# Products of constants in TensorE's waits, in the prologue and in the last sequence's expert part

## What is computed

```python
x = x + attn(layernorm(x));  x = x + ffn(layernorm(x))

def attn(x):                                     # linear-attention form with decays and levels
    q, k, v = (x @ W.T).reshape(b, t, H, 128)    # for Wq, Wk, Wv
    g = -softplus(x @ Wg.T + bg);  lam = softplus((x @ Wdl.T) + Lparam)
    G = cumsum(g, axis=1)
    A = (q k^T / sqrt(128)) * exp(G_t - G_s) * lam[level(t - s)]      # s <= t
    out = (A @ v).reshape(b, t, H * 128) @ Wo.T + x
    return layernorm(out) * ln_g + ln_b

def ffn(x):
    gate = softmax(x @ Wg + bg); keep the two largest, divided by their sum
    return sum_e gate_e * (We[e] @ x + be[e])
```

## Time and profile before

| | |
|---|---|
| median of 3 runs | 1558.06 us (1557.87 to 1558.11) |
| profiled execution | 1560.17 us, its span 1558.40 us |
| TensorE busy (matmul) | 1448.6 us, 93% of the span |
| ScalarE, VectorE, GpSimd busy | 1164.9, 1024.3, 886.7 us |
| chain that ended last | TensorE 68%, ScalarE 11%, GpSimd 9%, VectorE 7% |

### The profile page before, as it was taken

One profiled execution on the slowest core, in us unless ns is written; L12 is line 12 of the kernel. 1 busy time (PEld: TensorE's weight loads), 2 busy tenths in 40 slices (PEclk: granted clock), 3 DMA queues, 4 the chain that ended last, 5 costly groups with the idle time before them and its releaser, 6 DMA issues.

```text
span 1558.4 us, 30902 instructions
## 1 busy us (share of the span) xinstructions
PE 1448.6 (93%) x10678; PEld 1215.9 (78%) x10678; DVE 1024.3 (66%) x2466; ACT 1164.9 (75%) x3355; POOL 886.7 (57%) x887
## 2 busy tenths in 40 slices
PE   5599999999999999999999999999999999999966
PEld 4488787878878888788878788787887878788853
DVE  5355656686656767577665866667666676666675
ACT  2588887796788777787678877788777887777730
POOL 2055457744585455944578455864558545694560
PEclk8699999999999999999999999999999999999986
DMA  5310211111110111101111011111111011111100
GB/s 181 62 10 16 40 17 31 14 25 37 10 34 16 24 36 37 17 7 39 24 34 16 16 30 23 37 17 22 37 25 19 16 26 20 37 17 17 23 8 14
DMA packets 256470, 44.12 MB, mean 28 GB/s; under 512 B 197960, under 2 KB 254650, under 8 KB 256186
## 3 DMA queue, kind: packets, MB, share of 16 engines
q1 hardware_dynamic: 255468, 41.90, 14.3%
q10 hardware_dynamic: 846, 0.25, 0.1%
HBM read 32.38 MB, written 9.18 MB: 27 GB/s over the span
## 4 chain that ended last, share of the span: by engine, by line
PE 68%; ACT 11%; POOL 9%; DVE 7%; issue 2%; DMA 1%; SPq 1%; ACTq 0%; POOLq 0%; DVEq 0%
PE o_ps L1300 18%; PE l_ps L1231 9%; PE s_ps L1215 7%; PE s_ps L1217 7%; PE s_ps L1216 7%; PE aux L1215 5%; PE aux L1216 5%; PE aux L1217 5%; ACT w_all L695 4%; POOL a_lo L579 4%; ACT a_hi L717 2%; POOL yn L604 2%; DVE a_all L892 1%; PE o_ps L1295 1%; DVE z L968 1%
## 5 line engine op out<-in xcount | busy, mean ns | idle before, releaser
L579 POOL TENSOR_TENSOR a_lo<-a_all,a_hi 128x512 fp32r<-128x512 f32 (+2 forms) x640 | 710.1, 1125 | 573.5 <-ACT a_hi L717 570.6
L695 ACT ACTIVATE w_all<-l_ps,bias 128x128 f32<-128x128 f32 x2304 | 629.2, 387 | 50.8 <-PE l_ps L1231 49.8
L892 DVE TENSOR_TENSOR a_all<-s_ps,w_all 128x512 f32<-128x512 f32 (+3 forms) x768 | 423.4, 554 | 360.8 <-PE s_ps L1217 345.7
L717 ACT ACTIVATE a_hi<-a_all 128x512 fp32r<-128x512 f32 (+2 forms) x640 | 363.3, 591 | 202.3 <-DVE a_all L892 200.0
L1300 PE MATMUL o_ps<-a_hi,v_all 128*128 128x512 f32 (+2 forms) x1280 | 469.3, 371 | 16.2 <-POOL a_lo L579 15.7
L1215 PE MATMUL s_ps<-q_hi,xt_hi 128*128 128x512 f32 (+3 forms) x768 | 287.7, 375 | 5.6 <-DVE a_all L892 5.5
L1300 PEld LDWEIGHTS o_ps<-a_hi,v_all 128*128 128x128 f32 x1280 | 243.2, 190 | 61.5 <-POOL a_lo L579 29.8
L1217 PE MATMUL s_ps<-q_hi,xt_lo 128*128 128x512 f32 (+3 forms) x768 | 267.5, 348 | 0.0
L1216 PE MATMUL s_ps<-q_lo,xt_hi 128*128 128x512 f32 (+3 forms) x768 | 267.2, 348 | 0.0
L1300 PE MATMUL o_ps<-a_lo,v_all 128*128 128x512 f32 (+2 forms) x640 | 232.3, 363 | 0.0
L1231 PE MATMUL l_ps<-rb,mask 96*128 96x112 f16 (+4 forms) x1792 | 145.5, 221 | 23.4 <-ACT w_all L695 23.4
(11 more groups left out here) (176 smaller groups left out, 2037.8 us busy)
## 6 DMA issues: line engine op xcount, KB each, us to landing
rb<-eb_scratch SPq DMA_DIRECT2D x1016, 0.8 KB
ra<-ea_scratch SPq DMA_DIRECT2D x512, 4.0 KB, 2.0
mt<-m_scratch SPq DMA_DIRECT2D x62, 128.0 KB, 2.1
nt<-n_scratch SPq DMA_DIRECT2D x62, 128.0 KB, 2.6
tx<-in_L_attn_x SPq DMA_DIRECT2D x9, 512.0 KB, 4.4
out<-yn SPq DMA_DIRECT2D x16, 256.0 KB, 2.7
yx<-in_L_attn_x SPq DMA_DIRECT2D x7, 512.0 KB, 4.2
ea_scratch<-tx SPq DMA_DIRECT2D x15, 128.0 KB
```

The lines of the kernel that those rows point to most:

```text
L579: pool.tensor_tensor(a_lo[r][:, 0:t1 - t0], a[r][:, 0:t1 - t0], a_hi[r][:, 0:t1 - t0].bitcast(F32), ALU.subtract).then_inc(a_lo_done, 1)
L695: last = act.activation(w[k][:, W_AT[j] + dd, :].rearrange("p (f c) -> p f c", f=2), l_tiles[:, :, :, i - i0], ACT.Exp, bias=bias[b % 2][: ...
L717: act.activation(a_hi[r][:, 0:t1 - t0], a[r][:, 0:t1 - t0], ACT.Copy).then_inc(a_hi_done, 1)
L892: dve.tensor_tensor(a[(n * NG + g) % NA][:, 0:t1 - t0], s_ps[:, g % 2, 0:t1 - t0], w[n % 2][:, at:at + (t1 - t0) // P, :].rearrange("p i n ...
```

## The change

TensorE issues further products of `negm` and the first 64 columns' part of `identb`, 512 columns wide, in twelve places of the prologue and in four of the last sequence's pieces. Each writes `l_ps[:, 1, :]` or `s_ps[:, 1, :]` with `start=True`; nobody reads them. The wait for `s_consts` moves ahead of the first block, and a wait for `s_wetc` is added behind unit 0. A wait for the last `a_done` is added ahead of the last pieces.

```diff
+                def keep_busy(o, count):
+                    for _ in range(count):
+                        pe.matmul(o, negm[:, :], identb[:, 0:HF, :], start=True, stop=True, skip_group_check=True)
...
                 turn_level_weights()
+                pe.wait_ge(s_consts, 3)
+                keep_busy(l_ps[:, 1, :], 6)
                 pe.wait_ge(s_ones, 2)
                 pe.wait_ge(s_row, 16 * 6)
                 spread_rows()
+                keep_busy(l_ps[:, 1, :], 6)
                 for f in range(2):
                     turn_x(0, f)
...
                 turn_out_weights()
+                keep_busy(l_ps[:, 1, :], 6)
                 pe.wait_ge(ready, 2)
                 decay_sums(0)
+                keep_busy(l_ps[:, 1, :], 6)
                 for f in range(2):
                     turn_logs(0, f)
+                keep_busy(l_ps[:, 1, :], 4)
                 for u in range(Q_U):
                     query(0, u)
                 value_weights()
+                keep_busy(l_ps[:, 1, :], 5)
                 turn_expert_weights()
+                keep_busy(l_ps[:, 1, :], 8)
                 pe.wait_ge(mask_in, 16)
-                pe.wait_ge(s_consts, 3)
                 for u in range(NU):
                     unit(0, u)
+                    if u == 0:
+                        pe.wait_ge(s_wetc, 2)
+                        keep_busy(s_ps[:, 1, :], 20)
                     if u < NV:
                         value(0, u)
+                        keep_busy(s_ps[:, 1, :], 6)
...
+                pe.wait_ge(a_done, NH * NG)
+                idle = {("Y", 1): 30, ("X", 0): 8, ("X", 1): 5, ("H", 1): 12}
                 for kind, n, i in LAST_PIECES[1:]:
                     piece(kind, n, i)
+                    keep_busy(s_ps[:, 1, :], idle.get((kind, i), 0))
```

## The result

The changed kernel took **1555.12 us** (median of 22 runs, 1550.87 to 1557.59), the kernel before on the same chip 1558.49 (22 runs, 1556.32 to 1560.88). The ratio is 0.9979, with a 95% interval of 0.9973 to 0.9985: 3.4 us or 0.21% faster, at the edge of what I had called measurable. Forecast were 6.4 us. The time lies inside the range, but 3.4 us above the forecast, and little more than half of the forecast gain came.

What follows compares the result with a forecast made beforehand. TensorE at full clock bounds the middle; at both ends it waits and runs mostly at half clock. Terms +0.3 − 0.46 − 2.56 − 0.46 − 3.2 sum to −6.4 us, giving 1551.7 us; range 1549.2 to 1556.0.

Steps and rivals of the forecast that it cites:

- the prologue: Start of the span: first blocks +0.3 us, token transposes −0.46, token logits −2.56, filler among the units −0.46.
- the end: Last sequence: second-norm transpositions, gate logits and expert pieces run at a higher clock, −3.2 us together.
- rival 1: Prologue: the clock rises too late for the token logits, gain only 3.4 us, time 1554.7 us; chance 20%.
- rival 2: Last sequence: the clock falls again between 1519 and 1529 us, gain only 3.7 us, time 1554.4 us; chance 15%.
- The two transpositions and the gate logits: Last sequence, second norm and gate: full clock gives −0.46 us for each transposition and −1.7 for the gate logits.
- the 1.13 us: Last sequence: VectorE's three waits for expert pieces; about half was forecast won, −0.6 us, with ends at 0 and −1.13.
- the hand-over and the middle: Clock falls at 77 us and ahead of unit 3 in middle sequences: 0 taken for both; middle range ±2.0 us.
- unit 3: Prologue units: it takes 0.72 us instead of 1.03, and ScalarE's 0.16 us wait at unit 2 goes: −0.46 us.
- That leg of 21 us: Prologue, 36.3 to 57.45 us: SyncE's queue stores and reloads level logs and stores weights; earlier gains move it all forward.
- The logits: Prologue: 24 token-logit products at full clock take 2.72 us instead of 5.14, −2.56 us with the last one's length.
- rival 3: Prologue units: half-level clock when unit 1 is issued makes filler the bound, +6.8 us, up to 1561.5 us; chance 5%.
- rival 5: More than the sum: one middle fall fewer or none at 77 us, and all of the 1.13, 1548.7 us; chance 10%.

Runs made afterwards that it cites:

- mid_and_end: Kernel before plus six products in each of seven middle waits and the change's last-sequence blocks, none in the prologue: 1544.6 us, ratio 0.9911.
- end_only: Changed kernel without the 85 filler products of the prologue, keeping the 55 of the last sequence: 1555.9 us, ratio 0.9976 to the kernel before.
- prologue_only: Changed kernel without the 55 filler products of the last sequence, keeping the 85 of the prologue: 1560.24 us, ratio 1.0005 to the kernel before.
- mid_and_prologue: Kernel before plus six products in each of seven middle waits and the change's 85 prologue products, none at the end: 1548.2 us, ratio 0.9932.
- all_waits: mid_filler plus 40 narrow products behind the last expert piece and more filler in four further waits: 1541.73 us, ratio 0.9892 to the kernel before.
- all_waits_2: all_waits without the 20 and the four sixes among the prologue's units and without the 40 trailing products: 1540.83 us, ratio 0.9889 to the kernel before.
- longer_list: Changed kernel plus 40 products of 8 columns behind the last expert piece: 1556.37 us, ratio 0.9986 to the kernel before.
- mid_filler: Changed kernel plus six products in each of the seven middle waits ahead of unit 3: 1544.33 us, ratio 0.9908 to the kernel before.
- without_30: mid_filler without the block of 30 ahead of the second norm's transposes: 1545.51 us, ratio 0.9917 to the kernel before.
- fewer_ahead: Changed kernel without the block of 4 ahead of query 0 and the block of 5 behind the value weights: 1553.44 us, ratio 0.996.

## Where the prediction failed, and where it was right

The sum failed at the prologue, 3.2 of its 6.4 us; the 3.2 at the end came. Profile against profile 4.1 us were won. The runs show 3.4, since I had assumed the profiled execution 2.1 us above the median afterwards, and it stood 1.0 above. That the time still lies in the range is luck: the range was wide for rivals 1 and 2 and for falls in the middle, and rival 1's 1554.7 is near, but the loss came mostly by another way.

**Right: the end.** Forecast −3.2, measured −3.8 in the profile, −2.6 and −3.0 in the two comparisons of runs (mid_and_end, end_only). The two transpositions and the gate logits came as worked out. At the block of 12 this profile gave all of the 1.13 us and not half, because the clock fell at 1526.8, in the stretch of rival 2, but behind the gate products, where nobody waits for TensorE. In four of the seven profiles it went as the prediction describes: a wait of 2.5 us (forecast 2.8) stayed empty, a fall followed, and part of the 1.13 was lost.

**Right: the hand-over and the middle.** The fall at 77 us came again, at 76.1, and the six in the middle stayed, at 2 us each.

**Wrong: the prologue**, forecast −3.2, measured −0.4 at unit 3 and −0.3 at the last sequence in the profile, and nothing in the runs (prologue_only, 1.0005; mid_and_prologue, +1.0). Three steps failed.

1. "That leg of 21 us is DMA issue and landing. TensorE cannot shorten it, but whatever is gained before 27.25 us moves all of it forward." TensorE cannot shorten the leg, but its instruction list can lengthen it. 61 products ahead of value 0 bring a fetch forward, into the last store, and 1.7 us of the 1.9 that had reached SyncE went there, the rest in the first store, which had a fetch in it before as well. The sum had put nothing for this.

2. The logits, "24 × 0.214 = 5.14 us become 24 × 0.113 = 2.72". They took 3.79 (16.62 to 20.41 us), because the clock fell during them. I had only asked whether it would rise in time, and rival 1 had it too late; it rose in time and did not stay. Of the eight profiles whose list is that of the change up to the logits, five fell at 17 to 19 us as here, two had them at half level throughout, in one the clock held; with the wait ahead of them filled (all_waits, all_waits_2) it held.

3. "At full level a value (0.7 us) and six (1.3) end before ScalarE frees the next bank. Unit 3 takes 0.72 us in the middle". In this trace it had its size (−0.44 against −0.46), but not in general: in prologue_only, longer_list, mid_filler and without_30 ScalarE waited 1.8 to 2.1 us at unit 3 for filler at half level, and leaving these blocks out made mid_filler 2 to 3 us faster (with the fetch out of the store; the runs do not part the two). I had seen that danger only as rival 3, from a clock that stands low when unit 1 is issued. It was up then, and fell 0.2 to 1.5 us after TensorE had started on unit 2, in prologue_only in the block behind value 2 and in the three others ahead of it. Ahead of unit 2 TensorE had waited 2.4 to 2.6 us for ScalarE, 1.6 before, since at full level it arrives sooner.

Two side figures do not follow from the terms either: the signs for SyncE's store (33.3) and ScalarE's copy (54.4) are 3.0 us ahead, where the sum gives the prologue 2.7 up to there, and rival 5's 1548.7 is none of its sums (1549.2 with one fall fewer, 1549.9 with none at 77 us, 1547.9 with both).

The Trainium skill (TensorE: Matmul & The Clock Gate, Part 4), which says that transposes do not count for the clock as matmuls do, is not settled here. The clock held over the transposes at 1519.61 and 1522.55 us, with blocks of filler between them, and fell at 18.1, behind transposes, a 1.07 us wait and narrow products.

**Open.** What sets the time of a fetch to the microsecond: nine products less and forty more moved it the wrong way or hardly. Why prologue_only's other runs are 4 us above its profiled one. Part of the spread of runs is the number of falls in the middle (six in the profiles of before and after, three in end_only, whose profiled run was its fastest); at 2 us each they move a time by more than the whole change did. What decides whether the 1.85 us wait brings a fall in a given sequence was not found, beyond that filling it removed all.

## What to carry to other kernels

Count the clock's falls over the whole span before filling waits: one wait that returns in every sequence was worth 11 us, all the filler of both ends 3.4. Fill a wait only where the block ends before the next needed product even at the low clock, or where a long wait ahead of it has already brought the clock back. A leg that consists of DMA is not fixed: instructions added to an unrolled list bring fetches of the list forward, and a store in which a fetch began landed 1.1 to 1.8 us later.

## What the runs showed of the hardware that I had not expected

- An instruction fetch of 16 KB that begins inside a DRAM store delays its landing far beyond its own share (1.1% of 16 engines in the leg of 5.2 us): 3.44 to 3.47 us became 4.95 to 5.20, and 2.0 became 3.2 to 3.7. Behind the fetch of 0.93 us 11 packets of the store were left, which took 0.6 us more. Where the store's last packet had gone before the fetch (fewer_ahead), nothing was lost.
- The granted clock fell from 2.4 to 1.2 GHz while TensorE issued without a gap: at 18.1 us in products of 104 columns, 1.5 us behind a wait of 1.07 us, and at 1526.8 us behind 16 products of 8 and 16 columns.
- The same instruction list gave different clocks in different executions: with twelve dense products ahead of them the logits ran at full, mixed or half level.
